# Cross-attention with a residual and layer norm on one core: loads ahead of copies in SyncE's queue, the input's split last on ScalarE, normalisation a slot later

## The reference

```python
Q = split_heads(query @ Wq + bq)
K = split_heads(key @ Wk + bk)
V = split_heads(value @ Wv + bv)
scores = jnp.einsum('bhqd,bhkd->bhqk', Q, K) / np.sqrt(D_K).astype(np.float32)
attn = jax.nn.softmax(scores, axis=-1)
ctx = jnp.einsum('bhqk,bhkd->bhqd', attn, V)
ctx = ctx.transpose(0, 2, 1, 3).reshape(B, S, D_MODEL)
out = ctx @ Wo + bo
return _layer_norm(out + query, ln_gamma, ln_beta)
```

## Time and profile before

| what | value |
|---|---|
| median of 3 runs | 716.09 us (712.96 to 720.47) |
| profiled execution | 716.47 us |
| its span, first to last instruction | 714.7 us |
| mean granted TensorE clock | 0.966 |
| PE busy | 631.0 us (88%) |
| DVE busy | 544.0 us (76%) |
| POOL busy | 450.4 us (63%) |
| ACT busy | 365.8 us (51%) |

### The profile page before, as it was taken

The page is one execution under the profiler, slowest core; times in us unless marked ns, Lnnn a source line. Parts: engine busy times, 40 slices in busy tenths (PEclk is TensorE's granted clock), DMA queues, the critical chain, the costliest instruction groups (busy, mean ns, idle before and its releaser), DMA issues.

```text
span 714.7 us, 12042 instructions
## 1 busy us (share of the span) xinstructions
PE 631.0 (88%) x3336; PEld 430.6 (60%) x3336; DVE 544.0 (76%) x971; ACT 365.8 (51%) x667; POOL 450.4 (63%) x399
## 2 busy tenths in 40 slices
PE   6988967989898899999999989899989998998791
PEld 5966644666565656565665666566656565665470
DVE  4543265869797788888888888898889887887766
ACT  4611044456465566555656656565556565654541
POOL 1421023457676677776776777677767677765697
PEclk9999996999999999999999999999999999998996
DMA  9763567576777777778777776878677767675712
GB/s 321 283 203 84 148 175 181 146 167 172 185 190 179 187 181 188 190 183 199 197 173 194 177 194 180 212 186 201 178 191 190 193 186 190 170 174 146 213 60 88
DMA packets 93393, 129.58 MB, mean 181 GB/s; under 512 B 49937, under 2 KB 49937, under 8 KB 93361
## 3 DMA queue, kind: packets, MB, share of 16 engines
q1 hardware_dynamic: 93360, 129.19, 69.1%
HBM read 53.94 MB, written 24.35 MB: 110 GB/s over the span
## 4 chain that ended last, share of the span: by engine, by line
SPq 32%; PE 15%; DMA 12%; DVE 11%; issue 10%; POOL 8%; ACT 4%; ACTq 0%; DVEq 0%; POOLq 0%
SPq L539 18%; DMA xt<-in_x_t 10%; SPq L517 8%; PE p_o L658 5%; DVE part L811 4%; PE p_q L594 3%; SPq L475 3%; ACT qh L731 2%; DVE ql L860 2%; POOL y L961 2%; DMA xn<-in_x 2%; PE p_a L610 2%; POOL y L965 2%; PE p_s L624 2%; PE p_o L98 2%
## 5 line engine op out<-in xcount | busy, mean ns | idle before, releaser
L716 ACT ACTIVATE prob<-p_s 77x512 f32<-77x512 f32 x256 | 143.3, 586 | 50.5 <-PE p_s L624 48.7
L811 DVE TRANSPOSE_TENSOR_REDUCE part<-prob 96x64 f32<-96x2048 f32 x64 | 146.9, 2296 | 1.2 <-ACT prob L716 1.1
L868 DVE TENSOR_REDUCE nm<-p_a 128x4 f32<-128x308 f32 x256 | 115.7, 474 | 34.8 <-PE p_a L610 28.5
L610 PE MATMUL p_a<-kb,qh 128*128 128x308 f32 x256 | 86.2, 340 | 32.4 <-ACT qh L731 23.6
L951 POOL TENSOR_TENSOR xl<-xt,xh 128x512 fp32r<-128x512 f32 x60 | 77.2, 1287 | 58.8 <-ACT xh L723 58.8
L970 POOL TENSOR_TENSOR cl<-cxt,ch 128x512 fp32r<-128x512 f32 x64 | 82.5, 1289 | 47.4 <-ACT ch L741 47.4
L961 POOL TENSOR_TENSOR y<-y,gamma_row 128x512 f32<-128x512 f32 x60 | 76.6, 1276 | 52.5 <-ACT y L753 52.5
L977 POOL TENSOR_TENSOR xn<-xn,bo_row 128x512 f32<-128x512 f32 x60 | 77.4, 1290 | 45.1 <-DMA xn<-in_x 45.1
L624 PE MATMUL p_s<-z,ks 97*77 97x512 f32 x256 | 98.5, 426 | 7.6 <-issue 5.9
L594 PE MATMUL p_q<-xh,wqh 128*128 128x512 f32 x256 | 102.4, 400 | 1.7 <-PEq L150 1.7
L594 PE MATMUL p_q<-xl,wqh 128*128 128x512 f32 x256 | 102.2, 399 | 0.0
(11 more groups left out here) (123 smaller groups left out, 994.8 us busy)
## 6 DMA issues: line engine op xcount, KB each, us to landing
z<-qh SPq DMA_DIRECT2D x256, 128.0 KB, 2.3
xt<-in_x_t SPq DMA_DIRECT2D x64, 256.0 KB, 3.6
z<-ql SPq DMA_DIRECT2D x128, 128.0 KB, 2.3
xn<-in_x SPq DMA_DIRECT2D x60, 256.0 KB, 3.2
out_dram<-y SPq DMA_DIRECT2D x60, 256.0 KB, 3.3
ks<-k_high SPq DMA_DIRECT2D x32, 154.0 KB, 3.6
cx<-in_ctx_t SPq DMA_DIRECT2D x4, 616.0 KB, 5.4
k_high<-kth SPq DMA_DIRECT2D x4, 616.0 KB, 3.6
```

Of the source, the lines that this page charges most:

```text
L610: nc.tensor.matmul(p_a[t % 2][:, 0:HC * S2], qh[:, g.k // 2 % 2, g.k % 2, P * t:P * (t + 1)], kb[g.k // NCH % 2][:, g.k % NCH, :], start=T ...
L716: nc.scalar.activation(prob[0:S2, j, :], p_s[j % 2][0:S2, :], ACT.Exp, scale=SCALE).then_inc(prob_ready, 1)
L811: nc.vector.tensor_reduce(part[:], prob[0:KP, :, :].rearrange("p h (i r) -> p (h i) r", r=DK), AX_X, ALU.add, apply_transpose=True).then_i ...
L868: nc.vector.tensor_reduce(nm[:, t, g.k % 2:HALF:2], p_a[t % 2][:, 0:HC * S2].rearrange("p (h k) -> p h k", k=S2), AX_X, ALU.max, negate=Tr ...
```

## The change

It has four parts, all of order. No instruction is added or removed.

1. **SP**: in slot(g), the load of xn and the store of tile g-11 come ahead of the twelve z copies of an odd slot.
2. **ACT**: split_x_high(g+4) moves from the first to the last place of the slot (only the two splits of Wo stand behind it). normalize takes tile g-10 instead of g-9 (LAG_NORMALIZE = 10).
3. **DVE**: minus_mean_over_std takes tile g-10 and stands behind sum_keys, ahead of add_residual and q_low, instead of last.
4. **POOL**: scale and shift take tile g-11 (LAG_SCALE = 11), and inverse_std(g-9) comes behind ctx_low(g-4). The lists after the loop take up what the longer lags leave.

```diff
--- before.py
+++ after.py
@@ -42,7 +42,8 @@
 LAG_PV = 4
 LAG_OUT = 8
 LAG_NORM = 9
-LAG_SCALE = 10
+LAG_NORMALIZE = 10
+LAG_SCALE = 11
 LAG_STORE = 11
 WO_SLOTS = (3, 5)
 
@@ -529,6 +530,15 @@
                     load_kb(g.back(1 - NCH))
                 if g.back(LAG_LOAD_X).valid(NG):
                     load_xt(g.back(LAG_LOAD_X))
+                m = g.back(LAG_NORM - 2)
+                if m.valid(NS):
+                    if m.is_first():
+                        sp.wait_ge(wo_low, KC)
+                        sp.wait_ge(wo_high, KC)
+                    all_at_least(sp, (squared, m.over(1, -1)))
+                    sp.dma_start(xn[:, m.k % 2, :], x_dram[m.over(1)]).then_inc(xn_in[m.k % 2], 16)
+                if g.back(LAG_STORE).valid(NS):
+                    store(g.back(LAG_STORE))
                 if g.k % 2 == 1 and g.back(1).valid(NG):
                     c = g.back(1)
                     i = c.k // 2 % 2
@@ -538,13 +548,6 @@
                         for j in range(HC):
                             sp.dma_start(z[DK * part:DK * (part + 1), i, j, :, :].bitcast(F32),
                                          src[DK * j:DK * (j + 1), i, :, :].bitcast(F32)).then_inc(z_in[i], 16)
-                m = g.back(LAG_NORM - 2)
-                if m.valid(NS):
-                    if m.is_first():
-                        sp.wait_ge(wo_low, KC)
-                        sp.wait_ge(wo_high, KC)
-                    all_at_least(sp, (squared, m.over(1, -1)))
-                    sp.dma_start(xn[:, m.k % 2, :], x_dram[m.over(1)]).then_inc(xn_in[m.k % 2], 16)
                 if last_batch_chunk(g, 1) == NCH - 2:
                     for t in range(QT):
                         if t == 0:
@@ -553,8 +556,6 @@
                         if t == 2:
                             sp.wait_ge(pv_summed, NG - NCH)
                         sp.dma_start(x_last[t], x_dram[NS + t]).then_inc(x_last_in[t], 16)
-                if g.back(LAG_STORE).valid(NS):
-                    store(g.back(LAG_STORE))
                 for i in v_in_slot(g.back(1)):
                     store_v(i)
                 if g.back(WO_SLOTS[0]).is_first():
@@ -762,8 +763,6 @@
 
             def slot(g):
                 s, v, m, n = g.back(LAG_SCORE), g.back(LAG_PV), g.back(LAG_NORM), g.back(LAG_SPLIT)
-                if n.valid(NG):
-                    split_x_high(n)
                 if g.valid(NG):
                     q_high(g)
                 if m.valid(NS):
@@ -773,13 +772,16 @@
                         exp(s, j)
                 if v.valid(NG):
                     ctx_high(v)
-                if m.valid(NS):
-                    normalize(m)
+                if g.back(LAG_NORMALIZE).valid(NS):
+                    normalize(g.back(LAG_NORMALIZE))
+                if n.valid(NG):
+                    split_x_high(n)
                 for kc in wo_in_slot(g):
                     split_wo_high(kc)
             run(act, slot)
+            normalize(Slot(0, NS - 2))
             square(Slot(0, NS - 1))
-            for m in range(NG + LAG_PV - LAG_NORM, NS + ON_POOL):
+            for m in range(NS - 1, NS + ON_POOL):
                 normalize(Slot(0, m))
 
         @block.vector
@@ -880,6 +882,8 @@
                 v, m = g.back(LAG_PV), g.back(LAG_NORM)
                 if v.valid(NG):
                     sum_keys(v)
+                if g.back(LAG_NORMALIZE).valid(NS):
+                    minus_mean_over_std(g.back(LAG_NORMALIZE))
                 if m.valid(NS):
                     add_residual(m)
                 if g.valid(NG):
@@ -894,8 +898,6 @@
                         row_maxima(g, t)
                     if g.k % 2 == 1:
                         turn_maxima(g)
-                if m.valid(NS):
-                    minus_mean_over_std(m)
                 for i in v_in_slot(g):
                     dve.wait_ge(v_summed, i + 1)
                     dve.wait_ge(v_stored[i % 4], 16 * (i // 4))
@@ -927,6 +929,7 @@
                                                op0=ALU.mult, op1=ALU.add).then_inc(y_last_done, 1)
 
             m = Slot(0, NS - 1)
+            minus_mean_over_std(Slot(0, NS - 2))
             add_residual(m)
             variance_of_squares(m)
             add_last(0)
@@ -989,10 +992,10 @@
                     split_x_low(n)
                 if b.valid(NS):
                     add_bo(b)
+                if v.valid(NG):
+                    ctx_low(v)
                 if m.valid(NS):
                     inverse_std(m)
-                if v.valid(NG):
-                    ctx_low(v)
                 t = last_batch_chunk(g, LAG_PV + 1)
                 if t is not None:
                     add_bo_last(t)
@@ -1003,20 +1006,22 @@
             run(pool, slot)
             add_bo_last(QT - 1)
 
-            last = [Slot(0, NS + t) for t in range(-2, QT)]
+            last = {t: Slot(0, NS + t) for t in range(-3, QT)}
+            scale(last[-3])
+            shift(last[-3])
+            inverse_std(last[-1])
+            scale(last[-2])
+            shift(last[-2])
+            inverse_std(last[0])
+            scale(last[-1])
+            inverse_std(last[1])
+            shift(last[-1])
+            inverse_std(last[2])
             scale(last[0])
-            inverse_std(last[1])
+            inverse_std(last[3])
             shift(last[0])
-            inverse_std(last[2])
             scale(last[1])
-            inverse_std(last[3])
             shift(last[1])
-            inverse_std(last[4])
-            scale(last[2])
-            inverse_std(last[5])
-            shift(last[2])
-            scale(last[3])
-            shift(last[3])
 
 
 def xattn(nc, a, out):
```

## The result

| | before | changed |
|---|---|---|
| median | 718.28 us (4 runs) | 924.43 us (4 runs) |
| ratio | 1 | 1.2871, interval 1.2779 to 1.2964 |
| span of the profiled execution | 714.7 us | 922.1 us |
| mean granted TensorE clock | 0.966 | 0.837 |
| residual add to residual add, mean of slots 9 to 60 | 9.51 us | 13.50 us |

The account below looks back on a forecast made before the run. A one-slot ring through PE, ACT, POOL and DVE was to bound the kernel: 12.0 us plus 1.25 for clock, taken as 13.2. 716.5 - 485.0 + 51 x 13.2 - 2 = 902.7, said as 900 us; range 835 to 965.

Parts of the forecast that it names:

- The ring: Closed chain through PE, ACT, POOL and DVE, from one slot's residual add to the next: 12.0 us a slot.
- The six terms: Residual add to ch 4.56, to xh's end 1.86, gap 0.08, xl to rstd 4.28, gap 0.04, nmr 1.17 us.
- the first term: Residual add to ch, through PE's p_o and scores and ACT's exps: 4.56 us.
- The port: On DVE, two-input nmr is shut out by POOL's SBUF-reading scale and takes 1.25 us.
- the race: Whether DVE's nmr or POOL's scale starts first; nmr winning: 0.16 us, ring 10.9, 785 or 836 us, 9 in 100.
- The clock: PE falls to half clock after 3.7 us waits, in about four slots of five, adding 1.25 us a slot.
- The ends: Slots 0 to 8 gain 2 us; after slot 60, 66 us for eight slots; POOL's longer tail taken as 0.
- the sum: Slots 9 to 60: 51 slots at 13.2 us, 673.2 us, within the whole kernel's 902.7.
- The signs: Slots alike at 12 us or more, nmr waiting 2 to 3 us, xh's load wait near 0, PE about 70%.
- Costed at nothing: On SP, z copies complete some 1 us later behind xn load and store; covered, so no cost taken.
- The faster rival: Ring not closed, rstd reaching nmr before DVE ends sum_keys: 8.5 us a slot, 663 us; 3 in 100.

Follow-up runs that it names:

- a3: Changed kernel with 28 extra, unread matmuls on PE between scores 1 and the first p_o in slots 9 to 60: 886.40 us, ratio 1.2321.
- a2: Changed kernel with nmr computed by a tensor_scalar, one tensor input in SBUF instead of two: 844.55 us, ratio 1.1743.
- b1: Kernel before with only the SP part of the change, xn load and store ahead of the twelve z copies: 716.79 us, ratio 0.9933.
- a1: Changed kernel with POOL's inverse deviation put back ahead of xl, add_bo and ctx_low: 740.73 us, ratio 1.0252.
- a8: Changed kernel with POOL reordered (inverse deviation, add_bo, then xl), one-input nmr, and x's split and load one slot further ahead: 656.67 us, ratio 0.9108.
- a4: Changed kernel with only ACT's split of x put back to the slot's start: 717.60 us, ratio 1.0003.
- a5: Changed kernel with add_bo moved ahead of xl on POOL: 799.23 us, ratio 1.1118.

## Why the prediction was right, point by point

- **The ring.** Its place and every link are as forecast. The six terms came to 12.0 us; at full clock the ring is 11.75 (a3), and slot 20 of the changed kernel took 11.77. In the turn shown above: ch to the end of xh 1.84 for 1.86, xl to rstd's end 4.26 for 4.28, nmr to the residual add 1.14 for 1.17. The quarter of a microsecond is in the first term: 4.37 in a3 for the 4.56 that I took from a slot in which PE did not start at once. 51 slots, -13 us.
- **The port.** nmr is held behind POOL's scale in 55 of the 60 tiles: 1.21 us is its median. The other outcome of the race was seen where the ring starts (0.16 us in slot 10). The page that the prediction cites, the Trainium skill, SBUF — State Buffer, section Who interferes with whom, also states that a DVE instruction with at most one SBUF input, outside the two-port modes, does not contend with GpSimd. The trace of a2 agrees: such an instruction took 0.21 us beside a running POOL operation.
- **The clock.** Right in kind, too small in size. I took 0.8 x 1.6 = 1.25 us a slot, from five waits in the trace of before, and rounded it to 1.2. Measured are 13.50 - 11.75 = 1.75 us a slot, 28 us more over the 51 slots. It comes in every slot from 10 to 59 but slot 20, and not in four of five: residual add to ch is 5.94, 5.82, 6.70 and 6.80 us in the four slots above, for 4.37 at full clock.
- **Missed: a second reader.** I followed xh and xl into the ring, and not to the other engine that reads them. p_q of a batch's first chunk needs xl of the last chunk, which the change makes at the end of the slot just before. Two sentences of the prediction do not hold: that PE's wait is in one piece between scores and p_o, and that a low stretch on p_q is not on the ring. In one slot of four the wait lies ahead of p_q, the half clock falls on p_q, and p_o is up to 2.5 us late. Slot 20 shows that the wait alone costs nothing there. The sum hardly moved by it: the twelve slots that begin a batch take 13.48 us in the mean, the other 39 take 13.51. What the closed ring would take without this reader, no run shows. The waits of the changed kernel have it on record, 15 batches of 16:

```profile
PE p_q L595 <- issue: 39.9, 15, 2.8
```

- **The ends.** Slots 0 to 8 gave nothing of the 2 us that I took off (the first residual add is at 143.20 for 142.79); the slots after 60 take 68.7 us for 66, and 0.9 more at the very end. Together some 6 us.
- **The 24 us.** The 51 slots take 688.7 us for the 673.2 of the sum, 15.5 more: 13 less for the ring and 28 more for the clock. The ends add 6, and 902.7 was rounded to 900. That the forecast came within 3% is in part luck, since its two errors have opposite signs.
- **The signs.** Seen as named: nmr's wait and its length, POOL's wait for xh, no wait of xh for its load, low clock in many slices. Not as named: slot 20 is 11.77 us and not over 12, the slots repeat in fours and not alike, and PE's share is 78% and not about 70, since slow matmuls count as busy (723.2 us for 631.0).
- **Costed at nothing, rightly.** The z copies: in the slot shown they start at 412.01, 1.3 us behind the end of q_low, and the chain of waits of the changed kernel has none of them. The xn load and the store ahead of them made the kernel before 0.7% faster by themselves (b1).
- **The faster rival** was put at 663 us for a ring that is not closed. With the ring opened and nothing else done the kernel takes 741 (a1), since the second reader's wait and DVE's 8.9 us stand next. 657 us took the further slot of lead and the one-input nmr (a8).

## What to carry to other kernels

When an order is changed in a pipeline of in-order engines, follow from one instruction through the queues until the same instruction of the next turn is met: if the way closes within one turn, the slot cannot be shorter than its sum, and no buffer or earlier load helps. Here that sum could be had from durations of the trace of before to 2% (12.0 for 11.75). Two moves (a split taken up last, an inverse taken up last) closed it together; with one of them undone the changed kernel was at most 2.5% slower than before (a1, a4), with both 29%. And for each value made later, look at all its readers: the second one's wait was hidden under the ring, and it cost 53 us with what followed it once the ring was open.

## What the runs showed of the hardware that I had not expected

- **A wait on PE can cost more than itself.** Taking 1.24 us out of the ring gave 2.36 us a slot (a5), taking 1.05 us out gave 1.46 (a2: 12.04 for 13.50), and 3.3 us of useless matmuls in each slot made the kernel 38 us faster (a3). The granted clock in the row of the windows, over the slots in the middle, is 0.82 in the changed kernel and 0.97 in a3 (stretch, its length, busy us of PE, PEld, DVE, ACT and POOL, clock, DMA share, GB/s):

```profile
150.00:800.00 650.00, 505.90 (x2308) 352.20 (x2307) 407.12 (x697) 258.35 (x480) 321.95 (x287) 0.82 0.52 132
```

```profile
150.00:800.00 650.00, 613.25 (x3861) 475.66 (x3860) 429.49 (x736) 271.53 (x505) 345.01 (x305) 0.97 0.54 138
```

The Trainium skill, TensorE: Matmul & The Clock Gate, Part 1, states that the array falls to half rate after idling; the trace agrees, with a pitch of 0.43 instead of 0.23 us behind waits of about 3 us. It did not follow every such wait: behind the 2.82 us at 282.17 the clock stayed up.
- **The price of a fall varies at one length of wait.** Behind 3.07 us it came with the first p_o (436.29) and lasted 5 us; behind 3.19 us it came 1 us later (410.85) and lasted 3.2 us. The slots were 2.3 and 1.5 us above 11.75.
- **The clock can cost where the wait does not.** The wait of 2.82 us ahead of p_q was hidden in the changed kernel both times; with half clock behind it the slot was 14.15 us, without it 11.77.
